# The second attention's probabilities turned in pieces of 128 columns and multiplied with block-wise value rows

## The reference

```
x = layernorm(x + attention(x))              # 16 heads of 64, causal, then a projection
x = layernorm(x + cross_attention(x, ctx))   # 16 heads of 16; ctx: 77 keys for each block of 256 tokens
x = layernorm(x + experts(x))                # top 2 of 8 experts, 256 -> 1024 -> 256, with a fallback expert
```

```
scores = Q K^T / sqrt(16)          # 256 x 77 for each of 16 heads
scores = where(mask == 0, -1e9, scores)
attn = softmax(scores);  out = (attn V) w_o^T
```

## Time and profile before

| | |
|---|---|
| Median of 3 runs | 1551.44 us (1550.63 to 1551.74) |
| Profiled execution, first to last instruction (its span) | 1547.9 us |
| PE matmuls busy | 1359.4 us, 88% of the span |
| PE weight loads busy | 1140.1 us, 74% |
| DVE busy | 1137.0 us, 73% |
| ACT busy | 925.7 us, 60% |
| POOL busy | 729.5 us, 47% |

### The profile page before, as it was taken

The page is one execution under the profiler, slowest core; times in us unless marked ns, Lnnn a source line. Parts: engine busy times, 40 slices in busy tenths (PEclk is TensorE's granted clock), DMA queues, the critical chain, the costliest instruction groups (busy, mean ns, idle before and its releaser), DMA issues. The chain is left out here.

```text
span 1547.9 us, 49899 instructions
## 1 busy us (share of the span) xinstructions
PE 1359.4 (88%) x17713; PEld 1140.1 (74%) x17713; DVE 1137.0 (73%) x3181; ACT 925.7 (60%) x2255; POOL 729.5 (47%) x923
## 2 busy tenths in 40 slices
PE   3599999999999999999999999864999999999940
PEld 2488888888888888888888887642688888888830
DVE  4678888888888888888888888748555555555538
ACT  3566777777777777777777756514344444444426
POOL 3135555564574575565566543420333334333326
PEclk9899999999999999999999999995999999999975
DMA  9667667667667666757666564019211411111135
GB/s 216 136 149 161 160 175 143 134 168 145 140 147 166 136 136 175 141 130 172 142 145 150 137 104 87 17 67 422 81 50 46 159 45 50 48 50 48 49 124 212
DMA packets 254604, 199.79 MB, mean 129 GB/s; under 512 B 180158, under 2 KB 212030, under 8 KB 251936
## 3 DMA queue, kind: packets, MB, share of 16 engines
q1 hardware_dynamic: 243328, 174.70, 47.2%
q0 software_dynamic: 6816, 17.71, 3.7%
q10 hardware_dynamic: 4224, 4.19, 0.8%
HBM read 93.79 MB, written 65.93 MB: 103 GB/s over the span
## 5 line engine op out<-in xcount | busy, mean ns | idle before, releaser
L1664 PE MATMUL ps_e<-xt,wres 128*128 128x128 f16 x3408 | 354.4, 220 | 0.6 <-issue 0.6
L1664 PEld LDWEIGHTS ps_e<-xt,wres 128*128 x3408 | 287.8, 98 | 72.6 <-issue 0.9
L1720 ACT ACTIVATE act_g<-ps_e,b 128x128 f32<-128x128 f32 x568 | 162.5, 369 | 223.9 <-PE ps_e L1664 115.8
L1671 PE MATMUL ps_e<-wres,g_hi 128*128 x568 | 214.5, 379 | 1.3 <-DVE g_lo L1750 1.3
L724 ACT ACTIVATE probs<-st_k,nmax 128x128 f32<-128x128 f32 (+1 forms) x512 | 199.9, 448 | 2.1 <-DVE nmax L931 2.0
L1623 POOL DMA_INDIRECT z_scr<-e_y,dst_i x71 | 83.5, 1176 | 220.5 <-DVE e_y L1741 220.5
L931 DVE CUSTOM_DVE_ANT_0 st_k<-ps,causal 128x128 f32<-128x128 f32 (+1 forms) x512 | 160.6, 351 | 32.6 <-PE ps L449 32.6
L731 ACT ACTIVATE pt_hi<-ps 128x384 f16<-128x384 f32 x256 | 125.0, 488 | 55.0 <-PE ps L457 31.5
L1673 PE MATMUL ps_e<-wres,g_lo 128*128 x568 | 154.8, 273 | 0.0
L1201 POOL TENSOR_TENSOR o_st<-o_norm,o_st 128x256 f16<-128x256 f32 x128 | 86.3, 674 | 127.2 <-ACT o_st L739 124.6
L936 DVE TENSOR_TENSOR pt_lo<-ps,pt_hi 128x384 f16<-128x384 f32 x256 | 141.3, 552 | 4.4 <-ACT pt_hi L731 1.9
(11 more groups left out here) (273 smaller groups left out, 4316.7 us busy)
## 6 DMA issues: line engine op xcount, KB each, us to landing
k_pair<-k_pair SPq DMA_DIRECT2D x96, 256.0 KB, 6.4
st_p<-in_moe_w SPq DMA_DIRECT2D x24, 768.0 KB, 5.8
w_scr<-st_p SPq DMA_DIRECT2D x24, 768.0 KB, 4.1
wres<-w_scr SPq DMA_DIRECT2D x18, 1024.0 KB, 19.7
v_scr<-v_tok SPq DMA_DIRECT2D x32, 512.0 KB, 3.7
v_pos<-v_scr SPq DMA_DIRECT2D x64, 256.0 KB, 6.2
q_st<-st_q SPq DMA_DIRECT2D x64, 128.0 KB, 3.4
z_scr<-zero SPq DMA_DIRECT2D x32, 256.0 KB, 3.6
```

The source lines that it names most:

```text
L1664: last = mm(out, w(c * FF + f * P, b, P), xt[:, t % 2, a, c], start=(m == 0), stop=(m == 5))
L1671: mm(out[:, 0:2 * D], g_hi[:, t % G_BUFS, f], w(KC * FF + f * D, 0, 2 * D), start=(f == 0), stop=False, skip_group_check=True)
L1720: nc.scalar.activation(act_g[:, k % 2, f], ps[:, 3 + 2 * (k % 2) + f // 4, (f % 4) * P:(f % 4 + 1) * P], ACT.Gelu, bias=bias[:, f:f + 1], ...
```

## The change

The padded 616 probability columns of a half (640 with zeros at the end) are cut into 5 pieces of 128 columns, whatever head they belong to, and 5 transposes of 128 x 128 take the place of 8 of 128 x 77. `pt2_hi` and `pt2_lo` become 128 partitions x 5 x 128 columns, and ACT and DVE take them from the banks as 384 and 256 columns. A piece spans 2 or 3 heads (2, 3, 2, 3, 2: 12 "head slots"), so row r of a piece has to meet the value row of the key and head that column r stands for, and zeros in the other heads of the piece. For that each block of tokens needs its values in this form, `v2_own`:

- PE `value_rows(t, cc)`: 5 products of `key_rows` (a constant of zeros and ones that copies key rows to their places) with the block's values `v2`, high and low parts side by side, 68 or 102 columns wide, into `c6`.
- ACT `value_rows`: copy of 128 x 408 from `c6` to `v2_rows`.
- POOL `own_values`: product of 128 x 408 with `slot_heads` (ones where the row belongs to the head), into `v2_own`.

All three are done twice for each block, in the block step. `pv2` then makes 3 products for each piece, 34 or 51 columns wide, that add up in `c7`. A function `value_constants` on POOL makes `key_rows` and `slot_heads` once, at the head of step 1, in 3 fills and 11 selects (one of 77 x 616, ten of 128 x 2 or 3; the second five, for the heads' other edge, are left out below). The additions to semaphores that nobody waits for are taken out everywhere.

```diff
+CHUNKS2 = (HB * CTX + P - 1) // P
+PADDED = CHUNKS2 * P
+FIRST_HEAD = [c * P // CTX for c in range(CHUNKS2)]
+HEADS_IN = [min(HB - 1, (c * P + P - 1) // CTX) - c * P // CTX + 1 for c in range(CHUNKS2)]
+BANK_CHUNKS = ((0, 1, 2), (3, 4))
...
@@ PE, stage_c @@
             if g == 2:
                 pe.wait_ge(s_x1, t + 1)
                 if p == 0:
-                    pe.wait_ge(s_kv2_lo, 2 * (half(t) + 1))
+                    pe.wait_ge(s_vrow_in, 2 * (half(t) + 1))
...
                 for j, bank in enumerate(banks2(t, cc)):
-                    for n in range(4):
-                        last = nc.tensor.transpose(bank[0:CTX, n * P:(n + 1) * P], probs2_of(t, cc)[:, 4 * j + n], ident[:])
+                    for n, c in enumerate(BANK_CHUNKS[j]):
+                        last = nc.tensor.transpose(bank[:, n * P:(n + 1) * P], probs2_of(t, cc)[:, c * P:(c + 1) * P], ident[:])
                     last.then_inc(s_t2, 1)
+        def value_rows(t, cc):
+            if t % 2:
+                return
+            b = half(t)
+            if cc == 0:
+                pe.wait_ge(s_kv2_lo, 2 * (b + 1))
+                if t == 0:
+                    pe.wait_ge(s_slots, N_SLOTS)
+            else:
+                pe.wait_ge(s_vrow_in, 2 * b + 1)
+            for c in range(CHUNKS2):
+                h, n, at = HB * cc + FIRST_HEAD[c], HEADS_IN[c], SLOT_AT[c] * 2 * (1 + DK)
+                last = mm(c6[:, at:at + n * 2 * (1 + DK)], key_rows[:, c * P:(c + 1) * P], v2[:, h:h + n].rearrange("p h k d -> p (h k d)"),
+                          start=True, stop=True)
+            last.then_inc(s_vrow, 1)
@@ PE, pv2 @@
-            for n in range(HB):
-                h = HB * cc + n
-                at = h * (1 + DK)
-                high, low = pt2_of(t, cc)
-                mm(c7[:, at:at + 1 + DK], high[:, n], v2_hi[:, h], start=True, stop=False, skip_group_check=True)
-                mm(c7[:, at + 1:at + 1 + DK], high[:, n], v2_lo[:, h], start=False, stop=False, skip_group_check=True)
-                last = mm(c7[:, at:at + 1 + DK], low[:, n], v2_hi[:, h], start=False, stop=True, skip_group_check=True)
+            if cc == 0 and even(t):
+                pe.wait_ge(s_vown, 2 * (half(t) + 1))
+            high, low = pt2_of(t, cc)
+            for c in range(CHUNKS2):
+                n, at = HEADS_IN[c], (HB * cc + FIRST_HEAD[c]) * (1 + DK)
+                out = c7[:, at:at + n * (1 + DK)]
+                v_hi, v_lo = (v2_own[:, cc, SLOT_AT[c]:SLOT_AT[c] + n, k] for k in range(2))
+                mm(out, high[:, c], v_hi, start=(c == 0), stop=False, skip_group_check=True)
+                mm(out, high[:, c], v_lo, start=False, stop=False, skip_group_check=True)
+                last = mm(out, low[:, c], v_hi, start=False, stop=(c == CHUNKS2 - 1), skip_group_check=True)
             last.then_inc(s_pv2, 1)
@@ PE, step: value_rows(s - 1, 0) behind pv(s, 0); value_rows(s - 1, 1) behind turn_probs(s, 1) @@
@@ ACT, step: value_rows(s - 1, 0) ahead of stage_d(s - 2, 1); value_rows(s - 1, 1) behind pt(s, 1) @@
+        def value_rows(t, cc):
...
+            act.wait_ge(s_vrow, 2 * b + cc + 1)
...
+            nc.scalar.activation(v2_rows[:, cc].rearrange("p s k d -> p (s k d)"), c6[:, 0:HEAD_SLOTS * 2 * (1 + DK)], ACT.Copy).then_inc(s_vrow_in, 1)
@@ ACT and DVE, stage_c: 384 and 256 columns for 512 and 512 @@
-                    nc.scalar.activation(pt2_of(t, cc)[0][:, 4 * j:4 * j + 4].rearrange("p h t -> p (h t)"), bank[0:CTX, :], ACT.Copy).then_inc(s_t2_hi, 1)
+                    first, n = BANK_CHUNKS[j][0], len(BANK_CHUNKS[j])
+                    nc.scalar.activation(pt2_of(t, cc)[0][:, first:first + n].rearrange("p c t -> p (c t)"), bank[:, 0:n * P], ACT.Copy).then_inc(s_t2_hi, 1)
@@ POOL @@
+        def value_constants():
+            pool.wait_ge(s_lo, len(CHUNKS))
+            for ins in (nc.gpsimd.memset(key_rows, 0.0), nc.gpsimd.memset(slot_heads[:], 1.0),
+                        nc.gpsimd.memset(probs2[:, HC:PADDED], 0.0)):
...
+            nc.gpsimd.affine_select(out=key_rows[:, 0:HC].rearrange("p (h k) -> p h k", k=CTX), in_=key_rows[:, 0:HC].rearrange("p (h k) -> p h k", k=CTX),
+                                    compare_op=ALU.not_equal, fill=1.0, base=0, pattern=[[0, HB], [1, CTX]], channel_multiplier=-1).then_inc(s_slots, 1)
+            for c in range(CHUNKS2):
+                at = slot_heads[:, SLOT_AT[c]:SLOT_AT[c] + HEADS_IN[c]]
+                begin = c * P - FIRST_HEAD[c] * CTX
+                nc.gpsimd.affine_select(out=at, in_=at, compare_op=ALU.is_ge, fill=0.0, base=begin, pattern=[[-CTX, HEADS_IN[c]]],
+                                        channel_multiplier=1).then_inc(s_slots, 1)
...
+        def own_values(t, cc):
+            if t % 2:
+                return
+            b = half(t)
+            pool.wait_ge(s_vrow_in, 2 * b + cc + 1)
+            if b >= 1:
+                pool.wait_ge(s_pv2, 2 * t)
+            nc.gpsimd.tensor_tensor(v2_own[:, cc].rearrange("p s k d -> p s (k d)"), v2_rows[:, cc].rearrange("p s k d -> p s (k d)"),
+                                    slot_heads[:].unsqueeze(2).to_broadcast([P, HEAD_SLOTS, 2 * (1 + DK)]), ALU.mult).then_inc(s_vown, 1)
@@ POOL, step @@
             if has(s - 1):
                 shift(s - 1, 0)
+                own_values(s - 1, 0)
             if has(s):
                 split_o(s, 1)
+            if has(s - 1):
+                own_values(s - 1, 1)
             if 0 <= s - 4 < PIECES:
                 piece_low(s - 4, 0)
...
-        run(step, {-1: constants})
+        run(step, {-1: constants, 1: value_constants})
```

More of the change, by code:

```diff
@@ L25 @@
 HB = P // DK
+CHUNKS2 = (HB * CTX + P - 1) // P
+PADDED = CHUNKS2 * P
+FIRST_HEAD = [c * P // CTX for c in range(CHUNKS2)]
+HEADS_IN = [min(HB - 1, (c * P + P - 1) // CTX) - c * P // CTX + 1 for c in range(CHUNKS2)]
+SLOT_AT = [sum(HEADS_IN[:c]) for c in range(CHUNKS2)]
+HEAD_SLOTS = sum(HEADS_IN)
+BANK_CHUNKS = ((0, 1, 2), (3, 4))
 E = 8
@@ L153, in attention_block @@
     k2_bd = sb("k2_bd", [P, 2, KC, HB, CTX], F16)
-    v2_hi = sb("v2_hi", [CTX, H, 1 + DK], F16)
-    v2_lo = sb("v2_lo", [CTX, H, DK], F16)
+    v2 = sb("v2", [CTX, H, 2, 1 + DK], F16)
+    late = {n: stage_x[n][:].rearrange("p c d -> p (c d)").bitcast(F16) for n in ("k", "v", "q")}
+    v2_rows, v2_own = (late[n][:, 0:2 * HEAD_SLOTS * 2 * (1 + DK)].rearrange("p (a s k d) -> p a s k d", a=2, s=HEAD_SLOTS, k=2) for n in ("v", "q"))
+    key_rows = late["k"][0:CTX, 0:PADDED]
+    slot_heads = sb("slot_heads", [P, HEAD_SLOTS], F16)
     sm = sb("sm", [P, 2, HB, CTX], F32)
@@ L202, in attention_block @@
     s_one = sem("s1_one")
+    s_vrow, s_vrow_in, s_vown, s_slots = (sem("s1_" + n) for n in ("vrow", "vrow_in", "vown", "slots"))
     s_xb, s_mv1, s_mv2 = sem("s1_xb"), sem("s1_mv1"), sem("s1_mv2")
@@ L610, in step @@
                 pv(s, 0)
+            if has(s - 1):
+                value_rows(s - 1, 0)
             if has(s - 2):
@@ L615, in step @@
                 turn_probs(s, 1)
+            if has(s - 1):
+                value_rows(s - 1, 1)
             if has(s + 1):
@@ L761, in stage_c @@
                         act.wait_ge(s_bd, 4 * half(t))
-                        act.wait_ge(s_pv2, 2 * t)
+                        act.wait_ge(s_vrow, 2 * half(t))
                     nc.scalar.activation(k2[:, 0], c6[:, 0:KC * CTX].rearrange("p (c k) -> p c k", c=KC), ACT.Copy).then_inc(s_kv2_hi, 1)
-                    nc.scalar.activation(v2_hi[:, :, 1:1 + DK], c6[0:CTX, 256:512].rearrange("p (h d) -> p h d", d=DK), ACT.Copy).then_inc(s_kv2_hi, 1)
+                    nc.scalar.activation(v2[:, :, 0, 1:1 + DK], c6[0:CTX, 256:512].rearrange("p (h d) -> p h d", d=DK), ACT.Copy).then_inc(s_kv2_hi, 1)
             if g == 2:
@@ L1582, in experts_block @@
     s_w = keep["s_w"]
-    s_held = keep["s_held"]
     xg = keep["xg"]
@@ L1685, in step @@
                 pe.wait_ge(s_g_lo, k - LAG + 1)
-                pe.sem_inc(keep["s_held_pe"], 1)
                 if k - LAG >= 2:
@@ L1736, in output @@
                 dve.wait_ge(s_sc[t % 2], 16 * (t // 2))
-            dve.sem_inc(keep["s_held_dve"], 1)
             nc.vector.scalar_tensor_tensor(out=y[:, t % 2], in0=ps_y[t % 2][:, D:2 * D], scalar=1.0 / (G_UP * WP_UP),
@@ L1896, in program @@
         }
-        for n in ("s_held", "s_held_pe", "s_held_act", "s_held_dve", "s_held_pool", "s_held_sp", "s_b", "s_x2_in"):
+        for n in ("s_b", "s_x2_in"):
             keep[n] = ctx.enter_context(nc.semaphore(n))
```

70 lines of the change are left out of this document (34 added, 36 removed).

## The result

The changed kernel takes 1532.49 us (median of 4 runs, 1530.81 to 1533.52), the kernel before 1551.04 us beside it (1550.09 to 1551.74): ratio 0.9877, with a 95% interval of 0.9863 to 0.9891. It is 18.6 us faster, where 8.7 were forecast. The profiled execution has a span of 1530.6 us against 1547.9, so 17.3 us are to be found in the trace.

The account below looks back on a forecast made before the run. It took the step as a loop of PE and POOL in turn, so only slots behind the last wait count. Plain steps -11.2, block steps 0, constants +4.0, end -1.5: -8.7 us, 1542.7; range 1530 to 1553.

Parts of the forecast that it names:

- the forecast's own part: Whole kernel: the prediction's main outcome, 1536 to 1548 us, chance 0.57.
- Rival A: All steps: PE's saved slots count in full, -24 us to 1527, or partly, 1530 to 1537; chance 0.19.
- block: the new work: Block step: ACT's v2_rows copy costs some 0.1 us; two own_values on POOL make shift 0.57 late.
- What does shorten POOL's queue are the additions that go: POOL ahead of shift: each removed addition saves 0.08 us, making a plain step 0.48 us earlier.
- so nothing new comes up: Behind the second transposes: ACT and DVE copy 640 columns, not 1024; shorter copies add no new wait.
- 1.19 us of cover: Block step: POOL's idle time before the second shift hides that much of own_values' 1.76 us.
- Rival C: Block step: both own_values unhidden ahead of shift, each block step +1.2, kernel +8 us, 1560; chance 0.11.
- Once: Head of step 1: POOL's value_constants take 4.0 us, PE stalls at value_rows; +4.0 us in all.
- The end: Last two tiles, a chain through all engines: two or three halves shorter on PE and ACT or DVE, -1.5 us.
- A's sign: Step lengths: both plain and block steps shorter by 0.8 us and more.
- B's premise: POOL's semaphore additions cost nothing, so the change evens out within 0.2%, 1552 us; chance 0.13.
- D's clock: PE's stall at value_rows drops the clock to half, some 2.5 us more, 1545; chance 0.4.

Follow-up runs that it names:

- drop_pool: The kernel before without the two semaphore additions in split on POOL, those on other engines kept: 1540.59 us, ratio 0.9929.
- before_no_adds: The kernel before with only the additions to the held semaphores left out, on all engines: 1534.06 us, ratio 0.9884.
- drop_dve: The kernel before without the additions in moments and predicated on DVE (four in a step), others kept: 1544.20 us, ratio 0.9952.
- pad_turn_second: The changed kernel with 8 transposes instead of 5 in the second half: 1541.23 us, ratio 0.9927.
- wide_act: The changed kernel with 8 transposes in both halves and ACT's copies back to 512 columns twice a half: 1546.56 us, ratio 0.9961.
- three pads: The changed kernel with 8 transposes in the first half, or 24 products in pv2 of one or the other half: 1532.62, 1534.60 and 1532.56 us.
- wide_both: The changed kernel with 8 transposes in both halves and both ACT's copies and DVE's subtractions at 512 columns twice: 1548.57 us, ratio 0.9976.
- own_apart: The changed kernel with the first own_values behind split_o(s, 1), the second where POOL is idle, PE waiting for each half's alone: 1525.27 us, ratio 0.9823.
- own_later: The changed kernel with the first own_values behind split_o(s, 1), both still ahead of the second shift: 1529.00 us, ratio 0.9850.
- const_early: The changed kernel with value_constants called in step 0 ahead of spread_k2(0, 0): 1528.66 us, ratio 0.9846.

## Why the prediction was wrong

It had the sign and, in its range of 1530 to 1553, the time, but its sum was 8.7 us where 18.6 were measured. That the range held the time was luck: 1532.5 is below the 1536 at which the forecast's own part began, and was covered only by Rival A, whose mechanism is not what happened. Term by term, us for a step:

| term | forecast | shown | by |
|---|---|---|---|
| plain: POOL's additions | -0.48 | -0.47 | drop_pool |
| plain: DVE's additions | none | -0.09 beside POOL's (-0.15 alone) | before_no_adds, drop_dve |
| plain: second transposes | -0.34 | -0.32 | pad_turn_second |
| plain: ACT's copies | 0 | -0.19 | wide_act |
| plain: first transposes, `pv2` of both halves | 0 | -0.02 to +0.02 | three pads |
| block: POOL's additions | -0.32 | -0.35 | drop_pool |
| block: DVE's additions | none | -0.31 beside POOL's (-0.34 alone) | before_no_adds, drop_dve |
| block: second transposes | -0.34 | -0.26 | pad_turn_second |
| block: copies | 0 | -0.17, ACT's 0.03 and DVE's 0.14 | wide_act, wide_both |
| block: the new work | +0.1 (ACT's `v2_rows`) and +0.57 | +0.80, of it 0.62 by the places of `own_values` | wide_both against before_no_adds; own_apart |

The shown terms add up to -1.07 and -0.29. (The prediction's -0.2 at the head of the block step is the -0.32 and the +0.1 in one.)

The first row agrees in part by luck. An addition costs 0.10 us on POOL and not 0.08, since the prediction took the time without one from the gap ahead of the subtraction (0.09) and not from that ahead of the cast (0.07); six of them are 0.62, of which the plain step gave back 0.47.

**The step that failed** is "What does shorten POOL's queue are the additions that go". The diff takes the same additions from `moments` and `predicated` on DVE, and the sum has no term for them, not even one of nothing. They stand between the statistics and their mean and ahead of the maxima, the very chain that the prediction named as the one for which POOL waits in a block step. Beside POOL's they are 0.31 us of each block step, 14 x 0.31 = 4.3 us, and 14 x 0.09 = 1.3 in the plain ones, together 5.6. That is most of the 8.6 us between the forecast -8.7 and the span's -17.3; counted by place, that difference is 14 x 0.27 in the plain steps, 14 x 0.29 in the block steps and 1.7 at the end, less 1.0 at the start.

**The second** is "so nothing new comes up" of the copies. It looked at those of the second half, behind the last wait. The first half's are ahead of `o_high` in ACT's queue, and so ahead of POOL's `split_o` and of the queue that the sum itself called the bound: 14 x 0.19 = 2.7 us. In the block step DVE's copies were the larger part of 0.17, 14 x 0.17 = 2.4 us. Against these three stand the new work and the second transposes of the block step, which came out worse than forecast by 0.13 and 0.08.

**`own_values`** had its price nearly right and its mechanism half. The 1.19 us of cover did not stay, as Rival C had feared: the maxima came 0.77 us later than in the kernel before without additions, 0.61 of it by the place of the first `own_values` (`own_later`). But POOL and DVE were late side by side, not one after the other, so the step paid once. All the new work was 0.80 for 0.67: besides the 0.62 of `own_values`, POOL's cast of the next tile comes 0.23 us later in the changed kernel's block steps than in `before_no_adds` (15.84 for 15.61 from the step's start), where the prediction had 0.1 for ACT's `v2_rows`. Only the additions kept the block step from getting longer.

**Once.** `value_constants`: +4.0 forecast, 4.42 shown by `const_early`. The end: -3.2 for -1.5. Of the -3.2, the last two steps are -1.7, and -0.7 of these come with the additions alone (`before_no_adds`). What lies behind them varies among executions by as much as is to be explained: all behind the 27 steps is 601.3 us before and 605.0 in `drop_dve`, which does less. So the end's causes stay open, and so does the +0.8 at the start, which lies between 79.8 and 83.4 us over the runs.

**The rivals.** 1532.5 lies where Rival A was put (1530 to 1537), and both kinds of step got shorter, the plain one by over 0.8, which is half of what the text had named as A's sign. A is wrong all the same: the pads give at most 0.02 us for three of its four kinds of slot. B's premise, that the additions are free, fell with `before_no_adds`. D's clock did fall to 0.50, and the stall's excess of 0.8 us bounds what that cost here.

"TensorE: Matmul & The Clock Gate" (the Trainium skill, section "LDWEIGHTS (loading the stationary operand)") would have had the loads of the transposes grow by 51/77. The trace after has 140 ns for 147, so the measurement decides against it, as the prediction took it.

## What to carry to other kernels

List every line of a diff by engine before the first sum, and price the same kind of line on each engine: the additions were costed on POOL from a row, and left out on DVE, where the same trace shows such a gap (505.87 to 506.01). An instruction that the profile doesn't count as busy, such as an addition to a semaphore, shows only as the distance from one instruction's end to the next one's start. When the time comes out where a rival had it, test the rival: putting the removed work back, one place at a time, told in four runs which slots had counted. A piece of work can be late twice over, in the other engine's queue and in its own, and curing one shows the other.

## What the runs showed of the hardware

An addition to a semaphore between a wait and the instruction behind it costs 0.11 us on DVE (0.14 against 0.03 between two instructions) and 0.10 on POOL (0.17 against 0.07); the ten on both engines in a plain step and the eight in a block step, with SP's, were worth 0.56 and 0.66 us, 1.2% of this kernel in all. "VectorE: DVE Perf Modes" (the Trainium skill, section "The DRAIN you can't avoid") has a semaphore after each DVE operation at no extra cost; the additions here were instructions of their own, between a wait and the next operation, and those were not free. Those on SP, ahead of DMA issues, showed no cost in the sum of the others.

Five selects on POOL over 128 partitions and 2 or 3 columns take 0.76 us, 0.15 each, and the 77 x 640 fill 0.64. PE's pause of 3.4 us was followed by some 3 us at a granted clock of 0.50 (1.2 GHz).
